# Output projection of a sandwich attention/FFN layer: both halves' transposes ahead of all four tiles, and two parts of the deferred tail two and four units later

## The reference

```
x = x + LN(attn(LN(x), wq, wk, wv, wo))        # 16 heads of 64, sliding window 256:
    # scores = q k^T / 8 over the block of 256 queries and 512 keys, band mask, softmax, @ v, @ wo.T
x = x + LN(sqrt(real^2 + imag^2))
    # real = LN(x) @ cos(theta + theta_noise),  imag = LN(x) @ sin(phi + phi_noise)
```

## Time and profile before

| | |
|---|---|
| runs of the kernel before | 4220.83 and 4064.22 us, median 4142.52 us |
| profiled execution | 4064.09 us; span of its slowest core (core 3) 4062.6 us |
| spans of the eight cores | 4046.2 to 4062.6 us |
| mean granted TensorE clock | 0.903 to 0.905 on cores 0, 1, 2, 6; 0.871 to 0.875 on cores 3, 4, 5, 7 (core 6: 0.904) |
| busy share, core 3 | PE 79%, DVE 41%, ACT 34%, POOL 3% |

### The profile page before, as it was taken

The page is one execution under the profiler, slowest core; times in us unless marked ns, Lnnn a source line. Parts: engine busy times, 40 slices in busy tenths (PEclk is TensorE's granted clock), DMA queues, the critical chain, the costliest instruction groups (busy, mean ns, idle before and its releaser), DMA issues.

```text
span 4062.6 us, 51931 instructions; the slowest of 8 cores (4046.2 to 4062.6 us)
## 1 busy us (share of the span) xinstructions
PE 3215.2 (79%) x19808; PEld 2115.0 (52%) x19808; DVE 1658.6 (41%) x3600; ACT 1368.1 (34%) x2176; POOL 111.7 (3%) x215
## 2 busy tenths in 40 slices
PE   0019888989888897979888898988889898888984
PEld 0016555556555555656555555655555566555552
DVE  2323335162634526263452516253351625335162
ACT  3433234232423424242332324242332424234231
POOL 1100000000000000000000000000000000000000
PEclk6557989989899898989899798989899898888987
DMA  6773331504233140423314140422315042331503
GB/s 210 248 267 126 125 144 43 207 21 174 97 125 145 56 194 26 187 78 125 145 72 177 63 193 36 166 104 117 141 54 207 22 167 103 125 138 50 207 11 135
DMA packets 54162, 511.25 MB, mean 126 GB/s; under 512 B 5792, under 2 KB 5920, under 8 KB 28576
## 3 DMA queue, kind: packets, MB, share of 16 engines
q0 software_dynamic: 30384, 266.35, 16.4%
q1 hardware_dynamic: 23536, 241.58, 16.3%
HBM read 465.97 MB, written 41.94 MB: 125 GB/s over the span
## 4 chain that ended last, share of the span: by engine, by line
PE 67%; DVE 20%; issue 5%; DMA 5%; ACT 3%; DVEq 0%; POOL 0%; SPq 0%; ACTq 0%; POOLq 0%
PE pb L517 34%; PE pb L461 17%; PE pb L670 5%; DVE attn_sb L701 5%; DVE stats L698 4%; PE pb L770 4%; PE pb L660 2%; DVE ao_sb L808 2%; PE pb L732 2%; DMA wsc<-pl 2%; PE pb L401 1%; DVE attnT_sb L743 1%; DVE sc L847 1%; DVE fml L424 1%; DVE fml L378 1%
## 5 line engine op out<-in xcount | busy, mean ns | idle before, releaser
L698 DVE TENSOR_REDUCE stats<-pb 128x1 f32<-128x384 f32 (+2 forms) x512 | 269.4, 526 | 820.9 <-PE pb L670 820.9
L770 PE MATMUL pb<-v_sb,attnT_sb 128*128 128x64 f32 x2880 | 483.0, 311 | 95.3 <-DVE attnT_sb L743 93.8
L770 PEld LDWEIGHTS pb<-v_sb,attnT_sb 128*128 128x128 f32 x2880 | 441.1, 227 | 170.1 <-issue 167.3
L712 ACT ACT_TABLE_LOAD x256 | 328.4, 1283 | 533.2 <-DVE attn_sb L701 532.9
L461 PE MATMUL pb<-fmh,slot0h 128*128 128x256 bf16 x1024 | 280.2, 274 | 264.8 <-DMA slot0l<-wsc 264.8
L517 PE MATMUL pb<-slot2h,fmh 128*128 128x512 bf16 x992 | 375.9, 379 | 13.4 <-ACT ao_sb L904 13.4
L517 PE MATMUL pb<-slot2h,fml 128*128 128x512 bf16 x992 | 375.9, 379 | 0.0
L517 PE MATMUL pb<-slot2l,fmh 128*128 128x512 bf16 x992 | 375.9, 379 | 0.0
L461 PE MATMUL pb<-fmh,slot1h 128*128 128x256 bf16 x960 | 276.8, 288 | 88.4 <-DVE sc L847 88.4
L701 DVE TENSOR_SCALAR attn_sb<-pb,stats 128x384 f32<-128x384 f32 (+2 forms) x512 | 303.6, 593 | 56.8 <-DVE stats L698 2.5
L732 PE MATMUL pb<-eyef_s,attn_sb 128*128 128x128 f32 x1440 | 291.9, 317 | 2.4 <-ACT attn_sb L712 2.4
(11 more groups left out here) (114 smaller groups left out, 4725.8 us busy)
## 6 DMA issues: line engine op xcount, KB each, us to landing
slot0h<-wsc SPq DMA_DIRECT2D x33, 2048.0 KB, 10.8
slot1h<-wsc SPq DMA_DIRECT2D x33, 2048.0 KB, 10.9
slot0l<-wsc POOLq DMA_DIRECT2D x33, 2048.0 KB, 13.0
slot1l<-wsc POOLq DMA_DIRECT2D x33, 2048.0 KB, 13.2
slot2h<-wsc SPq DMA_DIRECT2D x33, 2048.0 KB, 11.0
slot2l<-wsc POOLq DMA_DIRECT2D x33, 2048.0 KB, 13.0
x_sb<-x POOLq DMA_DIRECT2D x32, 512.0 KB, 6.2
y<-sc POOLq DMA_DIRECT2D x32, 512.0 KB, 3.1
```

Of the source, the lines that this page charges most:

```text
L698: ev[f"mx_{g}_{uu}"] = ve.inc(vector.reduce_max(stats[:, P + up:P + up + 1], kept, axis=AX.X))
L712: ev[f"ex_{g}_{uu}"] = ac.inc(scalar.activation(attn_sb[:, up * SL:up * SL + (c1 - c0 + 1) * 128], attn_sb[:, up * SL:up * SL + (c1 - c0 + ...
L770: ins = tensor.matmul(pb[b_av][:, (h % 8) * DH:(h % 8 + 1) * DH], lhsT, rhs, start=(first_in_bank and ci == 0), stop=(last_in_bank and ci ...
```

## The change

Two edits. In the output projection, the transposes of half 1 are emitted before the projection, and all four tiles are emitted in one call behind them and behind `emit_ln1(g + 1)`'s emission; tiles 0 and 1 still wait for the high and low parts of half 0, tiles 2 and 3 for those of half 1. The events that the copies at L847 and the split of `n3t` wait for are renamed accordingly. In the deferred tail `tail_c1` goes from unit 10 to unit 12 and `tail_c2` from unit 12 to unit 16. The helper loses its `tile0` argument.

```diff
-            o_use = 3 + 6 * g
-            _ow0 = [(ac, ev[f"aot0_{g}_hi"]), (ve, ev[f"aot0_{g}_lo"])]
-            emit_proj_tm(g, o_use, f"op0_{g}", None, None, [0, 1],
-                         tile_waits=[_ow0, _ow0],
-                         srch=fmh2, srcl=fml2)
-
             h_ev2, l_ev2 = emit_tsplit_tt(g, 1, ao_sb, f"aot1_{g}",
                                           waits=[(ve, ev[f"ao_{g}_1"])], banks=(2, 3),
                                           dsth=fmh2, dstl=fml2)
 
             if not last:
                 emit_ln1(g + 1, g_waits=[(mm, ev[f"aot1_{g}_tp1"])])
 
+            o_use = 3 + 6 * g
+            _ow0 = [(ac, ev[f"aot0_{g}_hi"]), (ve, ev[f"aot0_{g}_lo"])]
             _ow1 = [(ac, ev[f"aot1_{g}_hi"]), (ve, ev[f"aot1_{g}_lo"])]
-            emit_proj_tm(g, o_use, f"op1_{g}", None, None, [2, 3],
-                         tile_waits=[_ow1, _ow1], tile0=2,
+            emit_proj_tm(g, o_use, f"op_{g}", h_ev2, l_ev2, [0, 1, 2, 3],
+                         tile_waits=[_ow0, _ow0, _ow1, _ow1],
                          srch=fmh2, srcl=fml2)
...
-                    otag = f"op0_{g}" if ti < 2 else f"op1_{g}"
-                    kb.wait(vector, mm, ev[f"{otag}_mm{ti % 2}"])
+                    kb.wait(vector, mm, ev[f"op_{g}_mm{ti}"])
...
-            pending_tail[0] = [(2, tail_a), (6, tail_b), (10, tail_c1),
-                               (12, tail_c2)]
+            pending_tail[0] = [(2, tail_a), (6, tail_b), (12, tail_c1),
+                               (16, tail_c2)]
```

More of the change, by code:

```diff
@@ L484, in emit_proj_tm @@
         def emit_proj_tm(g, use_id, tag, hi_ev, lo_ev, banks, extra_waits=(),
-                         srch=None, srcl=None, tile_waits=None, kc_tag=None,
-                         tile0=0):
+                         srch=None, srcl=None, tile_waits=None, kc_tag=None):
             si = use_id % 3
             for ti, b in enumerate(banks):
-                tt, nh = (tile0 + ti) // 2, (tile0 + ti) % 2
+                tt, nh = ti // 2, ti % 2
                 @block.tensor
@@ L520, in _ @@
                     ev[f"{tag}_mm{ti}"] = mm.inc(ins)
-            ev[f"use_mm_{use_id}"] = ev[f"{tag}_mm{len(banks) - 1}"]
+            ev[f"use_mm_{use_id}"] = ev[f"{tag}_mm3"]
         nuse = 0
@@ L888, in build_nc @@
                                        banks=(4, 5, 6, 7),
-                                       hi_waits=[(mm, ev[f"op1_{g}_mm1"])],
+                                       hi_waits=[(mm, ev[f"op_{g}_mm3"])],
                                        dsth=fmh2, dstl=fml2)
```

## The result

Median of 11 runs 3984.6 us (3960.5 to 4264.2); ratio to the kernel before 0.9779, 95% interval 0.9749 to 0.9809: clearly faster, but whether by more than 2% is open. The forecast was 4007 us (ratio 0.986), range 3968 to 4045.

A forecast was written before the change was run, and what follows sets the result against it. TensorE was taken to bound the projections, waiting on VectorE in the attention and between the two. 4062.6 - 65.8 - 6.8 + 5.3 + 10.6 = 4005.9 us of span, so 4007 us; range 3968 to 4045.

The forecast's parts named there:

- The pause behind tile 1: Output projection: half 1's transposes and the wait before tile 2 go, 4.11 us a block, 65.8 us less.
- The clock's falls in that pause: Output projection: in four of 16 blocks the removed pause lowered the clock, 1.7 us lost each; 6.8 us less.
- Tile 0 later: Output projection: eight more transposes ahead of tile 0 start it 0.65 us later, bounds 0 and 0.65 us.
- If the clock comes back at the same moment: Tile 0's delay falls at half speed, costing 0.33 us of full-speed work a block; 5.3 us more.
- The second edit: Attention: moving the tail costs 1.33 us in each of 8 blocks, 0 in the other six; 10.6 us more.
- `tail_c2`'s bare cost: Attention behind pair 16: 2.35 us of work less 0.68 us of idle VectorE, 1.67 us; upper bound 3.49 us.
- another slow stretch behind pairs 18 to 20: Attention: a slow stretch following pair 18 to 20 would show the forecast wrong; that pair was expected at about 5.7 us.
- the tail pays twice: Attention: `tail_c1` and `tail_c2` each open a slow stretch at 3.49 us; 25 us more, 4033 us; chance 0.20.
- the sum's case: Whole kernel: all priced gains and costs added, 4007 us, own range 3992 to 4022; chance 0.55.
- the kinder clock: `tail_c1` opens no slow stretch (25 us), projection clock returns 1.25 us earlier (10 us); 3972 us; chance 0.15.
- Slower than before: Attention: both moved tail pieces cost what `tail_b` does today, 72 us more, 4079 us; chance 0.06.
- a first edit that does nothing: The removed 4.11 us return as a wait at L401 or before the K projection, 4069 us; chance 0.04.

The follow-up runs named there:

- filler: The first edit alone plus 19 or 10 unread matmuls per block between tiles 1 and 2: 4048 to 4054 us with 19, 4018 and 4021 us with 10.
- the transposes behind tile 0: The first edit alone, but with half 1's transposes between tiles 0 and 1 in place of ahead of tile 0: 3999 and 4004 us.
- the extra transposes: Kernel before, plus half 1's transposes done once more, unused, ahead of tiles 0 and 1, with the real ones left behind tile 1: 4065.5 us.
- the copies first: The first edit alone, plus VectorE's four projection-tile copies ahead of the low parts of the next block's transposes: 3856 to 3865 us, ratio 0.9475.
- the first edit alone: Changed kernel with the new output projection order but the tail back at units 10 and 12: 3958 and 3968 us, ratio 0.975.

## Why the prediction was right, and where its size was off

**The pause behind tile 1** (4.11 us a block, -65.8 us): right. 96 matmuls run without a pause, and nothing came back later: the K wait is 5.89 us as it was.

**The clock's falls in that pause** (-6.8 us): right in kind. 1.5 slow matmuls a block are gone, 1.5 x 0.21 x 16 = 5.0 us on the mean of the cores.

**Tile 0 later**: forecast 0.65 us. Tile 0 starts 5.26 us after the first transposes in place of 4.76, both means over cores and blocks: 0.50 us.

**"If the clock comes back at the same moment"**: this is the step that was mis-sized. The forecast put +5.3 us here for all 16 blocks and kept the earlier return for a rival. In fact slow matmuls in tiles 0 and 1 fell from 11.5 to 5.4 a block: 6.1 x 0.21 = 1.3 us a block, 21 us, less 16 x 0.50 = 8 us for the later start: -13 us where the sum had +5. It is shown on both sides: every kernel with the transposes in the wait has 3.6 to 6.5 slow matmuls a block there (seven kernels, the one that only adds them among them), every one without has 11.0 to 11.9 (three). The Trainium skill, page TensorE: Matmul & The Clock Gate, section "What's actually happening", says that activity releases the slow clock. By that rule work in the wait brings the clock back earlier, and the traces agree for these transposes; no run put other work into that wait. The rival had bounded this at 10 us, from a return 1.25 us earlier. Counted like it, from half 0's transposes, the return is 2.0 us earlier (7.7 in place of 9.7 us): at half speed 1.0 us a block, 16 us. The -13 above holds this gain and the later start together, at its price at the slow clock.

Together by these terms: 15 x (4.11 + 0.3 + 1.3 - 0.5) = 78 us for the projection stretch, measured 77.4.

**The attention untouched by the first edit**: not in the forecast, and the step that was left out. The first edit gave 15.3 us there (1191.0 to 1175.7) and 6 us between K and the next attention. The code there is the same. With the tail at the same places the attention is at 1194 with filler, at 1185.5 with the transposes behind tile 0, at 1184.5 with the extra transposes and at 1165.0 with the copies first. So a few us of work or pause outside move the attention by up to 29 us. The intervals show where, with the tail at 10 and 12: whether `tail_c2` is followed by 6.49 and 5.16 us or by 5.58 and 4.08. The second kind appears in 42 of the 112 full blocks of all cores with the first edit alone, in 8 of 112 before: 34 x 1.99 us over 8 cores are 8.5 of the 15.3 us. The granted clock over pairs 14 to 18 is 0.89 in blocks of the second kind and 0.65 in the others (first edit alone), so a fall or no fall of the clock goes with the difference. The total time at the low clock doesn't settle it: the attention spends 340 us at 1.2 GHz with the first edit alone and 341 with the extra transposes, which take 9 us longer. Why a given block gets the one or the other kind stays open, beyond that it changes with what stands elsewhere in the block. In some kernels all cores come to the same attention from different starts (with the extra transposes 1183.7 to 1185.6 us, their first transposes at 391 to 413 us), in the changed kernel they don't (1177.6 to 1198.5 us).

**The second edit** (+10.6 us): it costs time, as forecast, but its size is not settled and its mechanism was not the forecast one. Alone it is +8.5 us (ratio 1.0021) on the slowest core, +5.8 on the mean of the eight cores' spans (4055.8 against 4050.0 us, four and eight runs). On top of the first edit the one profiled execution has +10.3 us in the attention (1186.0 against 1175.7), but the mean of the cores' spans over nine and two runs is 3952.4 against 3949.7 us, +2.7, and the ratios 0.9779 and 0.975 have intervals that touch. The first interval fell by 0.86 us (forecast 8 x 0.34 and 6 x 1.66 over 14 = 0.91). `tail_c2`'s bare cost was put at 1.67 us in a stretch that `tail_c1` had already slowed; the two intervals behind it rose by 1.04 + 0.40 = 1.4 us. What the forecast named as a sign of being wrong, another slow stretch behind pairs 18 to 20, is there. In the changed kernel, block 6 of core 3, the pairs 16 to 22 open like this:

```profile
1738.47 0.85 PE L659 MATMUL pb<-maskc_s,eyebf_s 128*128 128x384 bf16 x2
1743.63 0.48 PE L659 MATMUL pb<-maskc_s,eyebf_s 128*128 128x384 bf16 x2 [0.43 <-DVE attn_sb L700]
1749.21 0.80 PE L659 MATMUL pb<-maskc_s,eyebf_s 128*128 128x384 bf16 x2 [0.45 <-DVE attn_sb L700]
1755.30 0.85 PE L659 MATMUL pb<-maskc_s,eyebf_s 128*128 128x384 bf16 x2
```

The clock is back for pair 18 and falls again for 20 and 22. In 69 of the 112 full blocks it falls twice between pairs 14 and 24. So the mechanism of the rival that the tail pays twice came in most blocks, and only its price did not: beyond undisturbed pairs, pairs 12 to 24 cost 4.8 us a block with two slow stretches and 5.2 with one, against 4.1 with the first edit alone and 4.6 before. That the cost still came out near the forecast was luck: the reason given for it held in the fewer blocks.

**The rivals.** The outcome lies between the sum's case and the kinder clock: its second half (the clock back earlier in the projection) came, with more than the worth given; its first half (`tail_c1` without a slow stretch) did not: the intervals 14 to 18 are 5.93 and 5.07 us in the changed kernel (mean over full blocks and cores), 2.8 us above two undisturbed ones. Slower than before, and a first edit that does nothing, are excluded by the first edit alone.

**How much of it was luck.** By the mean of the cores' spans the first edit alone took 100 us (4050.0 to 3949.7), where its terms in the forecast add up to 67. The changed kernel lands near the 3972 us of the kinder clock, but 25 of that case's 35 us were to come from the tail, where they didn't, and the first edit gave some 21 us in stretches whose code is the same (15 in the attention, 6 from K on), for which the forecast had no term. The range held the result; the reasons given for its lower part only hold for the projection.

## What to carry to other kernels

Work that has to be done anyway is worth trying in a wait behind which TensorE's clock is low: here 8 transposes moved into such a wait brought back 1.3 us a block beside the pause they no longer cause, and moved one tile later they didn't. When a pause is removed, count the pauses that stay: with the first wait filled and the second left, the clock fell in the second one, and nothing was won. A wait that this change left was worth as much as all that it took: with the VectorE copies no longer queued behind work that waits for another engine, 100 us went, and the order of two emitted pieces did it.

## What the runs showed of the hardware

- Eight 128x128 float32 transposes of 1.94 us ahead of a run of dense matmuls shorten the low-clock stretch after it: granted clock over the first 5 us 0.52 and 0.53 without, 0.76 to 0.84 with them (means over all cores and blocks of six kernels).
- The same 3.07 us pause leaves the clock up or lets it fall, depending on what went before: it fell in 23 of 128 blocks of the kernel before and in 122 of 128 with the extra transposes ahead of tile 0.
- Adding 4.1 us of matmuls to a block cost 5.5 us (88 us over 16 blocks), and 2.2 us cost 3.7: in a kernel whose clock falls and returns in every block, the time wasn't the sum of its pieces to better than some 20 us.
- Block 0's first L352 transposes start 16 to 25 us apart on the cores of one execution; a change of a slowest core's span by that much says little by itself.
